# Attention, second pass: one exponential over two PSUM banks for the wide tiles

## The reference

```
energy = einsum('bhqd,bhkd->bhqk', q, k)            # 16 heads of 16 channels
energy = where(abs(q_index - k_index) > 128, fmin, energy)
att = softmax(energy / sqrt(256), axis=-1)
out = einsum('bhqk,bhkd->bhqd', att, v) @ Wp.T + bp
```

## Time and profile before

| | |
|---|---|
| median of 3 runs | 1384.45 us (1383.04 to 1385.96) |
| profiled execution | 1384.07 us |
| its span, first to last instruction | 1382.0 us |
| TensorE busy, share of the span | 1329.7 us, 96% |
| VectorE busy | 687.0 us, 50% |
| ScalarE busy | 488.3 us, 35% |
| GpSimd busy | 446.8 us, 32% |
| granted TensorE clock | 0.996 |

### The profile page before, as it was taken

The page is one execution under the profiler, slowest core; times in us unless marked ns, Lnnn a source line. Parts: engine busy times, 40 slices in busy tenths (PEclk is TensorE's granted clock), DMA queues, the critical chain, the costliest instruction groups (busy, mean ns, idle before and its releaser), DMA issues.

```text
span 1382.0 us, 25005 instructions
## 1 busy us (share of the span) xinstructions
PE 1329.7 (96%) x8348; PEld 1029.0 (74%) x8348; DVE 687.0 (50%) x2499; ACT 488.3 (35%) x1046; POOL 446.8 (32%) x541
## 2 busy tenths in 40 slices
PE   7899999999999999999999999999998999999998
PEld 5566556688999999755666666666665799999998
DVE  5655456233333333436888888888888231300000
ACT  2221211122222222122676676666766512111111
POOL 2100000253222222251554454544333534344332
PEclk9999999999999999999999999999999999999999
DMA  9402011067777777233555554655442789999996
GB/s 330 131 31 68 9 37 48 20 225 233 233 236 242 239 235 240 77 111 100 148 140 151 155 151 132 176 137 153 141 121 91 267 301 341 342 338 341 333 348 207
DMA packets 95676, 254.29 MB, mean 184 GB/s; under 512 B 12189, under 2 KB 42271, under 8 KB 85568
## 3 DMA queue, kind: packets, MB, share of 16 engines
q1 hardware_dynamic: 79728, 217.61, 48.5%
q0 software_dynamic: 12096, 32.13, 7.5%
q10 hardware_dynamic: 3728, 2.97, 0.7%
HBM read 201.42 MB, written 52.17 MB: 183 GB/s over the span
## 4 chain that ended last, share of the span: by engine, by line
PE 84%; DVE 8%; issue 4%; ACT 3%; DMA 0%; DVEq 0%; ACTq 0%; POOLq 0%
PE psum L994 10%; PE psum L675 10%; PE psum L1004 10%; PE psum L813 10%; PE psum L796 7%; PE psum L686 6%; PE psum L851 4%; PE psum L898 4%; PE psum L873 4%; PE psum L922 3%; DVE work L1892 3%; PE psum L823 2%; PE psum L768 2%; PE psum L933 2%; PE psum L956 2%
## 5 line engine op out<-in xcount | busy, mean ns | idle before, releaser
L1892 DVE CUSTOM_DVE_ANT_0 work<-psum,mask 128x384 bf16<-128x384 f32 (+1 forms) x512 | 230.0, 484 | 53.5 <-PE psum L851 52.2
L851 PE MATMUL psum<-kz,qT 96*128 96x384 f32 (+1 forms) x512 | 165.3, 391 | 14.2 <-DVE small L1892 12.9
L1971 POOL DMA_INDIRECT work<-normed,token_of x71 | 67.3, 948 | 323.6 <-PE psum L768 196.7
L675 PE MATMUL psum<-arena 128*128 128x512 f32 x320 | 147.5, 599 | 0.0
L994 PEld LDWEIGHTS psum<-arena 128*128 128x128 f32 x1248 | 145.5, 192 | 2.4 <-issue 0.4
L994 PE MATMUL psum<-arena 128*128 128x128 f32 x1248 | 146.1, 275 | 0.0
L813 PEld LDWEIGHTS psum<-work,arena 128*128 128x128 f32 x1136 | 134.9, 191 | 14.8 <-ACT work L1148 11.0
L813 PE MATMUL psum<-work,arena 128*128 128x128 f32 x1136 | 142.1, 278 | 3.6 <-ACT work L1148 2.0
L1244 ACT ACTIVATE arena<-psum 128x384 f32<-128x384 f32 x256 | 112.5, 496 | 85.4 <-PE psum L873 82.7
L1004 PE MATMUL psum<-arena 128*128 128x256 f32 x624 | 141.6, 379 | 0.8 <-issue 0.8
L873 PE MATMUL psum<-qT,kz 100*128 100x384 f32 (+1 forms) x512 | 131.9, 330 | 8.7 <-ACT arena L1244 8.4
(11 more groups left out here) (243 smaller groups left out, 1983.2 us busy)
## 6 DMA issues: line engine op xcount, KB each, us to landing
arena<-in_w SPq DMA_DIRECT2D x78, 1024.0 KB
arena<-in_wgu SPq DMA_DIRECT2D x71, 704.0 KB, 4.9
strips<-hi SPq DMA_DIRECT2D x64, 256.0 KB
kz<-strips SPq DMA_DIRECT2D x64, 192.0 KB, 3.2
qT<-strips SPq DMA_DIRECT2D x32, 384.0 KB, 4.7
results<-work SPq DMA_DIRECT2D x71, 128.0 KB
strips<-lo SPq DMA_DIRECT2D x32, 256.0 KB
normed<-work SPq DMA_DIRECT2D x14, 512.0 KB, 3.1
```

Source lines behind the costliest of these rows:

```text
L675: m = e.matmul(psum[0:w, bk, :], sgu[:, k, u, c * P:c * P + w], xnT_all[:, b, k, :], start=(k == 0), stop=(k == EC - 1))
L851: m = e.matmul(psum[:, bk, at:at + w], qT[0:ROWS_S, slot, half, i * P:(i + 1) * P], kz[slot][0:ROWS_S, hd, lo_key:hi_key], start=True, sto ...
L1892: e.tensor_tensor_reduce(masked[:, n % 2, 0:w], psum[:, bank_of["scores", u, i, hd], at:at + w], mask[:, P - off:P - off + w], 1.0, MASKED ...
L1971: e.indirect_dma_start(out=xs[:, b % 3, :], out_offset=None, in_=normed[l][0:n, :], in_offset=bass.IndirectOffsetOnAxis(ap=token_of[:, l, ...
```

## The change

For wide tiles the two exponentials of a half become one instruction that reads columns 0 to 383 of banks 3 and 4 and writes two heads of `pT`, as the narrow tiles' does from one bank. It waits for both matmuls and increments `p_exped` once. `exps_before` becomes two a tile for all tiles, so that both banks of a half are free with the same increment.

```diff
@@ -520,9 +520,7 @@
 
         def exps_before(u, j, hd):
 
-            wide = [window(n)[1] - window(n)[0] > 2 * P for n in range(TPB)]
-            per = [G if w else G // 2 for w in wide]
-            return u * sum(per) + sum(per[:j]) + (hd if j < TPB and wide[j] else hd // 2)
+            return G // 2 * (u * TPB + j) + hd // 2
 
         def m_ring(s):
 
@@ -1236,15 +1234,12 @@
             n = u * TPB + j
             if half == 0 and n >= 5:
                 e.wait_ge(*done["values", (n - 5) // TPB])
+            hd = 2 * half
             for i in range(2):
-                hd = 2 * half + i
-                bk = bank_of["again", u, j, hd]
-                e.wait_ge(*done["again", u, j, hd])
-                if w > 2 * P:
-                    e.activation(pT(u, j)[:, hd, 0:w], psum[:, bk, 0:w], ACT.Exp, scale=1.0 / E ** 0.5).then_inc(p_exped, 1)
-                elif i == 1:
-                    e.activation(pT(u, j)[:, hd - 1:hd + 1, 0:w], psum[:, bk, :].rearrange("p (h n) -> p h n", h=2), ACT.Exp,
-                                 scale=1.0 / E ** 0.5).then_inc(p_exped, 1)
+                e.wait_ge(*done["again", u, j, hd + i])
+            held = psum[:, AGAIN[0]:AGAIN[1] + 1, 0:w] if w > 2 * P else \
+                psum[:, bank_of["again", u, j, hd], :].rearrange("p (h n) -> p h n", h=2)
+            e.activation(pT(u, j)[:, hd:hd + 2, 0:w], held, ACT.Exp, scale=1.0 / E ** 0.5).then_inc(p_exped, 1)
 
         def act_place_maxima(e, u):
```

## The result

The changed kernel takes 1392.45 us (median of 5, 1391.95 to 1399.14) against 1385.75 us for the kernel before beside it. The medians differ by 6.7 us, the means by 9.5; the ratio, taken from all runs and not from the two medians, is 1.0070 with a 95% interval of 1.0051 to 1.0089, which is 7.1 to 12.3 us slower. Measured a second time it is 1397.67 us against 1383.33 us, ratio 1.0097 (1.0082 to 1.0112), the medians 14.3 and the means 13.4 us apart. The forecast was 1391.0 us, 6.6 more than before.

What follows compares the result with a forecast made beforehand. TensorE, busy 416 of attention's 440 us, was taken as the bound, with exponentials gating its matmuls. Terms 4.5 + 0.1 + 1.5 + 0.5 = 6.6 us on the profiled 1384.07, plus 0.4 for the median, gave 1391.0 us; range 1386 to 1396.5.

Steps and rivals of the forecast that it cites:

- Length of the pair: The new 768-column exponential on ScalarE takes 810 ns, saving 0.06 us a pair, 7.7 us in all.
- The gated place: Tile j = 1, between halves with narrow scores: first matmul to last takes 2.08 us instead of 1.80.
- 16 places on the chain, 0.28 each: Places where TensorE's own matmul starts the gating exponential each pay 0.28 us, 4.5 us in all.
- Queued places, + 0.0: Five places with ScalarE's queue ahead: gain and loss cancel, 0.0 each, 0.1 us put for all.
- Both gates at 669: Attention unit with both gates acting: + 0.40 us, 0.5 for the half behind; 1.5 us with the later unit at 1069.
- 25 halves with slack, cost nothing: Wide halves at tile j = 2: next L873 comes after 1.57 us, 1.47 needed; slack 0.10, no cost.
- TensorE's idle time before L873, "about 14 us": In attention, TensorE's idle time before the second pass's matmuls rises from 8.4 us to about 14.
- The sum: All terms in attention together: 4.5 + 0.1 + 1.5 + 0.5 = 6.6 us slower.
- The two other stretches as long as before.: Projections with routed experts (650 us) and the last experts (292 us) keep their length; only attention grows, some 6.6 us.
- A: ScalarE's queue sets the pace, each chain pair gives back 0.06 us: 1376.8 with all 128; chance 0.06.
- B: The 0.28 us delays go into TensorE's waits for VectorE: 0 to 2.7 us stay, 1384.5 to 1387.2; chance 0.17.
- C: Reading across two banks is slow, or the 0.10 slack is used up: 14.7 us, 1399, half gives 1395; chance 0.12.

Runs made afterwards that it cites:

- e3: Kernel before, both exponentials kept and each started by its own matmul, but only the second releases both banks; 4.7 us slower at equal clock.
- e4: Kernel before, each exponential still releasing its own bank, but the first waits for both matmuls; 5.4 us slower at equal clock.
- e2: Kernel before with one exponential for two heads only in tile j = 2; 3.2 us slower at equal clock.
- e1: Kernel before with one exponential for two heads only in tile j = 1; 9.0 us slower as timed, 5.7 at equal clock.
- e6: Kernel before with the transposes of the maxima moved ahead of the second pass's second half in the narrow-score step; 0.7 us of cost.
- e8: Kernel before with the maxima transposes moved ahead and one exponential for two heads only in tile j = 2; 4.3 us left at equal clock.

## Why the prediction was right, and where it was off

The direction and the mechanism held, and 1392.45 us lies within 1386 to 1396.5, 1.5 us from the 1391.0 forecast. That it lies so near is in part luck. The sum was too low: 6.6 us forecast, where the ratio gives 7.1 to 12.3 us and the second measurement 13.4, with a median, 1397.67, above the range. The first median comes from runs in which the clock, which the prediction leaves out, stood high. By its steps:

- *Length of the pair.* 810 ns from the slope, 811 measured. Right. The Trainium skill's 826 ns ("ScalarE: Activation LUTs", section on what ACT_TABLE_LOAD costs) is 15 ns high here, and ScalarE's saving was 8.6 us in all, 0.07 a pair, not its 0.09.
- *The gated place.* 2.08 forecast, 2.11 measured; of the 0.03 the hand-over to ScalarE has 0.02 (0.12, not 0.10). e3 and e4 took it apart: late release alone 1.98, late start alone 2.00, both 2.11.
- *16 places on the chain, 0.28 each.* The steps of 0.3 us in the middle of attention are these: 11 of them lie between the two reciprocals, 11 x 0.31 = 3.4 of the 4.12 us. Right, but for 0.03 a place.
- *Queued places, + 0.0.* There are six and not five; at 835 us stands one more of the same form. From the start of the first pair to the end of the matmuls 3.53 us before (776.57 to 780.10). After:

```profile
785.84 0.83 ACT L1242 ACTIVATE arena<-psum 128x768 f32<-128x768 f32 x1
786.70 1.20 ACT L1250 ACTIVATE qT<-psum 4x512 fp32r<-4x512 f32 x2
787.92 0.81 ACT L1242 ACTIVATE arena<-psum 128x768 f32<-128x768 f32 x1
...
788.78 0.62 PE L871 MATMUL psum<-qT,kz 100*128 100x384 f32 x2 [0.20 <-ACT arena L1242]
```

  785.84 to 789.40 is 3.56 us, + 0.03. Right: the faster first pair pays for the slower gate.
- *Both gates at 669.* From 668.59 to 673.89 it was 5.30 us, now 671.61 to 677.36 (676.74 + 0.62), 5.75: + 0.45 for 0.40 forecast. The half behind it stands 0.60 us, but the clock fell in that wait, so its price, 0.5 forecast, cannot be read off.
- *25 halves with slack, cost nothing.* Read off one row, and mis-sized. The usual ones did cost nothing (831.80 to 833.37 is 1.57 us again, with no wait), but others come onto the gate, 12 in the middle of attention in e2. There they cost 0.98 us. Over the whole kernel e2 gives 3.2 us for tile 2 at equal clock, where my terms that belong to it make 1.9 (0.1 at each of the 7 gates with ScalarE's queue ahead, when the pair of tile 1 before it is not there to pay for it; 0.5 + 0.2 behind them; 0.5 for halves off the chain).
- *TensorE's idle time before L873, "about 14 us".* 28.6, 20.2 more. By the place of the matmul in its unit, the second half of tile 1 went from 6.7 us in 25 places to 19.1 in as many; the first half of tile 2, which stands behind tile 1's last pair, from nothing to 2.4 us in 10; the places behind tile 2 from 1.6 us in 4 to 7.1 in 18. I had set down the price, 0.28 a place, where the row shows the standing, 0.52 more a place, and units that absorb it stand as long as the rest.
- *The sum.* 6.6 us forecast, 9.4 at equal clock. For the middle of attention the terms make 11 x 0.28 + 0.1 = 3.2 us, and two traces show 4.12 and 4.10. The other 3.4 us, for the two ends, were sized by hand from two places, and 5.3 are left for them. There the clock falls among the waits, and how the two share those microseconds is not shown.
- *"The two other stretches as long as before."* With few traces this cannot be judged: attention began 2.8 us later ahead of every changed instruction, and the stretch behind it gave back 1.5 us, as it did in the traces of e1 to e4 (1.2 to 1.5).
- *The clock.* Not in the prediction at all. In the second measurement 4.0 of the 13.4 us go with it. The changed order of work and a lower clock go together: nine of the ten experiments ran at a lower mean clock than the kernel before beside them, and the falls at 680 and 1050 us stand in the traces of the changed kernel and not in that of before. That the longer standing is what brings the clock down is likely and not shown (e6, with 0.7 us of cost, fell by 0.0036, e3, with 4.7, by 0.0005), and why one run of a kernel has more falls than another stays open.

The rivals: A (ScalarE's queue sets the pace) fell; no run got faster from ScalarE's shorter work. B (absorbed) holds in the late-L1904 units and for most of the new standing behind tile 2. Of C the slow read of two banks fell with the 811 ns; its other half, that the slack of 0.10 is used up, came true in those 12 places and not in the usual halves.

## What to carry to other kernels

Two buffers that are released one by one are a pipeline, two released together are one large buffer; joining their readers saves the fixed cost of an instruction on the reader (0.07 us here) and costs the writer its overlap at both ends (0.31 us here). It cost nothing where the writer had other work to the length of the whole read in between, as in the usual halves of tile 2. Where the reader's engine is the bound it may pay; no run here tests that. When the writer is the bound, look instead for work to put into its wait, one place at a time: here a delay mostly ran on in full, and a gain stopped at whatever was late next.

## What the runs showed of the hardware

An exponential that reads 384 columns from each of two neighbouring banks costs no more than its columns: 811 ns for 768, between 595 for 512 and 1023 for 1024. The mean granted clock of a whole execution moved between 0.986 and 0.996 with kernels that keep TensorE busy for 408 of 450 us (after) to 416 of 440 (before) in attention, and 0.001 of it went with 1.06 us of 1385. Small edits of the order of work went with a mean clock lower by up to 0.0064 (e8), 6.8 us, more than the 4.3 us that are left at equal clock; a comparison at 0.5% needs the clock beside each time.
